# An expert layer of a two-layer model on one core: all 15 row blocks loaded up front, three buffers for the copied weights

## The reference

```python
x = x + ga * _L1_attn_ref(h, ...)
h = _layernorm(x, axis=-1) * (1 + cb) + sb
# _L1_ffn_ref:
router_probs = softmax(xt @ Wr + br)
gates, idx = max(router_probs), argmax(router_probs)      # one of E = 8 experts per token
xn = (xt - mu) * rsqrt(var + LN_EPS) * ln_g + ln_b
h = relu(xn @ W1[idx] + b1[idx])                          # 128 -> 512
y = (h @ W2[idx] + b2[idx]) * gates                       # 512 -> 128
x = x + gb * y
```

## Time and profile before

| | us |
|---|---|
| median of three runs | 1146.57 |
| profiled execution | 1146.85 |
| its span, first to last instruction | 1145.0 |
| TensorE busy | 907.2 |
| DVE busy | 631.0 |
| ACT busy | 518.3 |
| POOL busy | 190.5 |
| first load of xb issued | 967.87 |
| first layer of block 2 / of block 14 starts | 985.77 / 1104.34 |
| first gather starts | 1118.51 |
| mean granted clock | 0.802 |

### The profile page before, as it was taken

One profiled execution on the slowest core, in us unless ns is written; L12 is line 12 of the kernel. 1 busy time (PEld: TensorE's weight loads), 2 busy tenths in 40 slices (PEclk: granted clock), 3 DMA queues, 4 the chain that ended last, 5 costly groups with the idle time before them and its releaser, 6 DMA issues. The chain is left out here.

```text
span 1145.0 us, 13297 instructions
## 1 busy us (share of the span) xinstructions
PE 907.2 (79%) x4532; PEld 524.6 (46%) x4532; DVE 631.0 (55%) x1354; ACT 518.3 (45%) x938; POOL 190.5 (17%) x161
## 2 busy tenths in 40 slices
PE   4559999999889999999968689689789961655550
PEld 2325555556557677776732223223323321555540
DVE  3326576866537675675686357577666514322222
ACT  1014545555557767665725345444444430433330
POOL 3625402121010000000022220010010013122215
PEclk9999999999999999999966556756655555766775
DMA  3414111111191000002112600300200000000003
GB/s 109 74 49 121 33 36 29 41 32 29 52 284 36 1 1 1 1 1 37 19 38 53 100 16 10 49 10 10 48 11 1 2 9 28 10 28 28 28 20 81
DMA packets 55647, 44.80 MB, mean 39 GB/s; under 512 B 5831, under 2 KB 46492, under 8 KB 55580
## 3 DMA queue, kind: packets, MB, share of 16 engines
q1 hardware_dynamic: 54555, 41.86, 15.3%
q0 software_dynamic: 1024, 2.10, 0.6%
HBM read 14.71 MB, written 14.55 MB: 26 GB/s over the span
## 5 line engine op out<-in xcount | busy, mean ns | idle before, releaser
L830 ACT ACTIVATE ring<-single 128x512 f32<-128x512 f32 (+3 forms) x512 | 249.9, 516 | 336.6 <-PE single L1031 190.6
L1445 DVE TENSOR_REDUCE mneg<-pair 128x2 f32<-128x1024 f32 (+3 forms) x256 | 259.5, 1022 | 125.0 <-PE pair L1031 66.6
L1031 PE MATMUL single<-q_op,k_op 26*128 26x512 f32 (+3 forms) x512 | 240.8, 570 | 55.0 <-ACT ring L830 31.8
L1031 PE MATMUL pair<-k_op,q_op 24*128 24x512 f32 (+3 forms) x512 | 210.9, 565 | 24.2 <-DVE mneg L1445 17.8
L1031 PEld LDWEIGHTS single<-q_op,k_op 122*128 122x128 f32 (+1 forms) x512 | 105.7, 237 | 168.3 <-ACT ring L830 82.7
L1088 PE MATMUL p_o<-ring,vaug 128*9 128x512 f32 (+3 forms) x1024 | 160.3, 707 | 1.2 <-ACT ring L830 1.2
L1500 DVE TENSOR_TENSOR ring<-ring,single 128x1024 f32<-128x1024 f32 x60 | 73.2, 1221 | 77.5 <-PE single L1143 62.2
L857 ACT ACTIVATE ring<-pair,cols 128x512 f32<-128x512 f32 x136 | 86.0, 685 | 63.9 <-PE pair L1132 62.4
L1031 PEld LDWEIGHTS pair<-k_op,q_op 120*128 120x128 f32 (+1 forms) x512 | 100.5, 246 | 30.8 <-DVE mneg L1445 23.2
L1505 DVE TENSOR_TENSOR hid_lo<-ring,hid_hi 128x1024 fp32r<-128x1024 f32 x68 | 83.2, 1224 | 10.4 <-ACT hid_hi L872 10.3
L872 ACT ACTIVATE hid_hi<-ring 128x1024 fp32r<-128x1024 f32 x68 | 72.1, 1060 | 12.4 <-issue 7.5
(11 more groups left out here) (286 smaller groups left out, 1412.1 us busy)
## 6 DMA issues: line engine op xcount, KB each, us to landing
xs<-zero SPq DMA_DIRECT2D x10, 1024.0 KB, 10.3
q_op<-hl SPq DMA_DIRECT2D x96, 64.0 KB
k_op<-hl SPq DMA_DIRECT2D x96, 64.0 KB
stage<-in_L_ffn_W_dram SPq DMA_DIRECT2D x8, 512.0 KB, 4.4
stage<-in_L_ffn_rW_dram SPq DMA_DIRECT2D x6, 512.0 KB, 5.8
xb<-xs SPq DMA_DIRECT2D x15, 128.0 KB, 2.0
xs<-yb SPq DMA_DIRECT2D x15, 128.0 KB, 1.7
qk_rope<-rope_hl SPq DMA_DIRECT2D x24, 64.0 KB, 2.0
```

Of the source, the lines that this page charges most:

```text
L830: exp_done.by(act.activation(ring[:, n % 8, lo:T], singles[n % 2][:, lo:T], ACT.Exp), (L, n))
L1031: ins = pe.matmul(dst[:, lo:hi], r32(lhs[:, lhs_lo:lhs_lo + P]), r32(rhs[:, lo:hi]), start=True, stop=L == 1)
L1445: s_taken.by(dve.tensor_reduce(mneg[:, G % 2, qt, 2 * p:2 * p + 2], pairs[m % 2][:, :, 0:hi], axis=AX.X, op=ALU.max, negate=True), (L, m))
```

## The change

SP issues the 15 loads one after another, each into its own part of a larger `xb` and with its own semaphore, and then the 15 stores. The copied weights and bias columns have three buffers in place of two; the third weight buffer lies on `hl`. Tiles at `at_op` move to other offsets, and `yg` moves to where the first rows were.

```diff
@@ placement
+        wst_at = cursor[0] - 8 * KB
-        b_blk = put("b_blk", [P, 2, 5])
+        b_blk = put("b_blk", [P, 3, 5])
-        wst = put("wst", [P, 2, 4, T], at=at_ring)
+        wst = [put("wst0", [P, 4, T], at=at_ring), put("wst1", [P, 4, T], at=at_ring + 8 * KB), put("wst2", [P, 4, T], at=wst_at)]
-        xb = put("xb", [P, 3, 2, D], at=at_op)
+        xb = put("xb", [P, NBLK, 2, D], at=at_op)
...
-        yg = put("yg", [P, NB, NT, D], at=at_op + 35 * KB)
+        yg = put("yg", [P, NB, NT, D], at=at_op)
-        xb_in, yb_out = [sem(f"xb_in{i}") for i in range(3)], [sem(f"yb_out{i}") for i in range(2)]
+        xb_in, yb_out = [sem(f"xb_in{i}") for i in range(NBLK)], [sem(f"yb_out{i}") for i in range(2)]
@@ SP
-            where = {}
-            for n in range(NBLK + 3):
-                if n < NBLK:
-                    where[n] = sp.value_load(btab[0:1, 0, n:n + 1], min_val=0, max_val=79)
-                    if n >= 3:
-                        xt_full.wait_ge(sp, n - 3)
-                    sp.dma_start(xb[:, n % 3, :, :].rearrange("p t d -> p (t d)").unsqueeze(1), blocks_of[:, bass.ds(where[n], 1), :]).then_inc(xb_in[n % 3], 16)
-                if n >= 3:
-                    m = n - 3
-                    yb_ready.wait_ge(sp, m)
-                    sp.dma_start(blocks_of[:, bass.ds(where[m], 1), :], yb[:, m % 2, :, :].rearrange("p t d -> p (t d)").unsqueeze(1)).then_inc(yb_out[m % 2], 16)
+            where = []
+            for n in range(NBLK):
+                where.append(sp.value_load(btab[0:1, 0, n:n + 1], min_val=0, max_val=79))
+                sp.dma_start(xb[:, n, :, :].rearrange("p t d -> p (t d)").unsqueeze(1), blocks_of[:, bass.ds(where[n], 1), :]).then_inc(xb_in[n], 16)
+            for n in range(NBLK):
+                yb_ready.wait_ge(sp, n)
+                sp.dma_start(blocks_of[:, bass.ds(where[n], 1), :], yb[:, n % 2, :, :].rearrange("p t d -> p (t d)").unsqueeze(1)).then_inc(yb_out[n % 2], 16)
@@ POOL
-                if n >= 2:
-                    y_full.wait_ge(pool, n - 2)
-                    yt_ready.wait_ge(pool, n - 2)
+                if n >= 3:
+                    y_full.wait_ge(pool, n - 3)
+                    yt_ready.wait_ge(pool, n - 3)
                     apart(pool)
-                pool.tensor_copy(b_blk[:, n % 2, :].unsqueeze(1), b_cols[:, bass.ds(e, 1), :])
-                w_here.by(pool.tensor_copy(r32(wst[:, n % 2, :, :].unsqueeze(2)), w_of[:, :, bass.ds(e, 1), :]), n)
+                pool.tensor_copy(b_blk[:, n % 3, :].unsqueeze(1), b_cols[:, bass.ds(e, 1), :])
+                w_here.by(pool.tensor_copy(r32(wst[n % 3][:, :, :].unsqueeze(2)), w_of[:, :, bass.ds(e, 1), :]), n)
@@ TensorE, rows_in
-                    pe.wait_ge(xb_in[n % 3], 16 * (n // 3 + 1))
+                    pe.wait_ge(xb_in[n], 16)
...
```

More of the change, by code:

```diff
@@ L319, in build @@
         k_op1 = put("k_op1", [P, 2, NG, T], at=at_op + 32 * KB)
-        xb = put("xb", [P, 3, 2, D], at=at_op)
[L321 to L327, removed]
-        yg = put("yg", [P, NB, NT, D], at=at_op + 35 * KB)
+        xb = put("xb", [P, NBLK, 2, D], at=at_op)
+        xt_hi = put("xt_hi", [P, 2, BLK], at=at_op + 15 * KB)
+        xt_lo = put("xt_lo", [P, 2, BLK], at=at_op + 17 * KB)
+        yt = put("yt", [P, 2, BLK], at=at_op + 19 * KB)
+        yb = put("yb", [P, 2, 2, D], at=at_op + 21 * KB)
+        hid1 = put("hid1", [P, 2, 4, BLK], at=at_op + 23 * KB)
+        hid1_hi = put("hid1_hi", [P, 2, 4, BLK], at=at_op + 31 * KB)
+        hid1_lo = put("hid1_lo", [P, 2, 4, BLK], at=at_op + 39 * KB)
+        yg = put("yg", [P, NB, NT, D], at=at_op)
         at_w = room(2 * 2 * CPR * P * 4)
@@ L902, in hidden @@
                         ins = act.activation(hid1[:, n % 2, c, :], pairs[n % 2][:, c // 2, BLK * (c % 2):BLK * (c % 2) + BLK], ACT.Relu,
-                                             bias=b_blk[:, n % 2, c:c + 1])
+                                             bias=b_blk[:, n % 3, c:c + 1])
                     relu_done.by(ins, n)
@@ L1188, in rows_in @@
                         lo = P * t
-                        ins = pe.transpose(singles[0][:, lo:lo + P], xb[:, n % 3, t, :], ident)
+                        ins = pe.transpose(singles[0][:, lo:lo + P], xb[:, n, t, :], ident)
                     xt_full.by(ins, n)
@@ L1200, in first_layer @@
                         dst = pairs[n % 2][:, c // 2, BLK * (c % 2):BLK * (c % 2) + BLK]
-                        hi, lo = (r32(wst[:, n % 2, half, P * c:P * (c + 1)]) for half in range(2))
+                        hi, lo = (r32(wst[n % 3][:, half, P * c:P * (c + 1)]) for half in range(2))
                         pe.matmul(dst, hi, r32(xt_hi[:, n % 2, :]), start=True, stop=False)
@@ L1212, in second_layer @@
                     for c in range(4):
-                        hi, lo = (r32(wst[:, n % 2, 2 + half, P * c:P * (c + 1)]) for half in range(2))
+                        hi, lo = (r32(wst[n % 3][:, 2 + half, P * c:P * (c + 1)]) for half in range(2))
                         pe.matmul(dst, hi, r32(hid1_hi[:, n % 2, c, :]), start=(c == 0), stop=False)
@@ L1553, in result @@
                     apart(dve)
-                    yt_ready.by(dve.tensor_scalar(yt[:, n % 2, :], (p_o, p_m)[n % 2][:, 0:BLK], b_blk[:, n % 2, 4:5], None, ALU.add), n)
+                    yt_ready.by(dve.tensor_scalar(yt[:, n % 2, :], (p_o, p_m)[n % 2][:, 0:BLK], b_blk[:, n % 3, 4:5], None, ALU.add), n)
                 low_rows(0)
```

## The result

The changed kernel takes **1074.18 us** (median of 3 runs, 1068.37 to 1074.76) against 1146.57 (1134.54 to 1147.28): ratio 0.938, 95% interval 0.928 to 0.949. Its profiled execution took 1074.18 us as well, 72.7 less than the one of before (1146.85), with a span of 1072.4. The forecast was 1078. Times here are medians of all executions of a kernel, and ratios leave out the slow executions, those more than 1.5% above its fastest.

What follows compares the result with a forecast made beforehand. Two waits ending within half a microsecond bounded layer 1's expert blocks: row loads behind late stores, and weight copies. 1146.85 less 3.8 (block 2), 64.3 (12 blocks) and 1.2 (tail) gave 1078 us; range 1064 to 1098.

Steps and rivals of the forecast that it cites:

- part 1: Loads on SP: 15 issues at most 1.14 us apart, no wait for rows left after the first.
- part 2: Three weight buffers: POOL's third copy no longer waits, first layer of block 2 starts at once, 3.8 us gained.
- either alone would give little: Expert blocks of layer 1: row and weight waits end within half a microsecond, so removing one gains little.
- part 3: Expert loop: POOL's copy holds up DVE's xt_lo in each block; 4.52 us a block, 12 blocks 64.3 us less.
- The rival without a lock: Expert loop: POOL's copy rarely holds up xt_lo; 3.94 us a block, 1071 us; chance 0.12.
- The clock: TensorE in the new loop: no idle over about 1.1 us, so 2.4 GHz from block 2 on.
- The low-clock rival: TensorE stays at or falls back to 1.2 GHz: 6.0 us a block, 1096 us; chance 0.18 including mixtures.
- The tail: Last first layer to the gather: one layer of 12 matmuls at the higher clock, 1.2 us less.

Runs made afterwards that it cites:

- lag5: w3_only with the store of block n-5, not n-3, behind the load of block n, still three row buffers: 1077.89 us, ratio 0.939 to the kernel before.
- w3_only: The kernel before with the change's three weight buffers, loads left where they stood: 1132.46 us, ratio 0.989 to the kernel before.
- no_copy: The changed kernel without the copy of block weights from block 3 on (blocks use old weights): 1065.51 us, ratio 0.931 to the kernel before.
- x15_only: The changed kernel with two weight buffers again, the 15 loads still up front: 1145.73 us, ratio 0.998 to the kernel before.
- w4_only: The changed kernel with a fourth weight buffer, xt moved elsewhere in SBUF: 1076.73 us, ratio 0.931 to the kernel before.
- w4_xt_psum: The changed kernel with xt kept in PSUM and a fourth weight buffer: 1069.13 us, ratio 0.933 to the kernel before.
- half_copy: The changed kernel copying only the first layer's weights from block 3 on: 1069.10 us, ratio 0.933 to the kernel before.

## Why the prediction was right

**The rows of the loads and their reach (part 1).** Right: no wait for rows but the first, and 15 issues 1.11 us apart (at most 1.14 was said). The last one was out by 981.8, before the first store had to go. lag5 adds what the step didn't claim: the queue's order was the cause.

**The first layer of block 2 (part 2).** -4.0 against -3.8, without an idle. What w3_only showed is that "either alone would give little" was too low for this one: I had priced the removed waits at block 2 and 14 by themselves, and not what comes sooner because of them.

**What is late next (part 3).** Right in mechanism and size: 4.52 a block, 12 blocks 54.26 us against 54.2. The single held xt_lo of the earlier trace rows was the only case of it in the trace; it held for 12 blocks because the order of copy and xt_lo is decided by yt, 0.81 and 0.96 after it. That the sum is met to a few hundredths is in part luck. In the block from 1015.77 on, the transposes start 0.15 behind xt_lo, the first layer 0.17 behind them and its last matmul 1.38 later, where the sum had 0.05, 0.30 and 1.31; these errors nearly cancel. The rival without a lock, 3.94 a block, is near what no_copy measured (3.86) with the copies out. The mean that was written for it was right, but not its even pace: in no_copy TensorE waits for hid_lo in every second block only, and the blocks take about 3.4 and 4.4 us in turn.

**The clock.** Right: 1.00 from 982 to 1036 with idles of about 1.1 us in each block. The low-clock rival needed 6.0 a block. In x15_only, with idles of 4.35 us, the clock was 0.75, and a first matmul took 0.55 instead of 0.38. So a part of the 64.3 us is the clock that came with the tighter loop: 24 matmuls a block all at 0.12, where part of them ran at 0.22. How large a part, no run separates.

**The tail.** Too small: -2.15 and not -1.2. I gave one layer back to the higher clock. The second layer of block 14, whose first matmul took 0.55 at 1111.50, took 0.38 at 1039.96 behind an idle about as long (2.42 and 2.16 us). What the engine had done before that idle differed: a 12-block loop at 1.00 here, a 5.00 us idle one layer earlier there. That this is the reason is argued, not shown.

**Not foreseen.** The stage began 2.0 us earlier though nothing ahead of it was changed. The total came out 3.8 us under the forecast: 2.0 of this, 1.0 of the tail, 0.2 each of the second and the last stretch, and 0.45 of rounding 1077.55 up to 1078.

## What to carry to other kernels

Before taking away the wait that a profile names, look for the one that ends just behind it: here each removal alone gave 0.2 or 1.1%, both 6.2%. A deep set of buffers can hide that only the order on one queue was wrong: a load should not stand behind a store whose data come so late that the load's rows are already wanted. In lag5 a store two blocks older in the same place cost nothing. When a loop gets tighter, find what then runs under a GpSimd copy on VectorE with two inputs in SBUF: moving one of them to PSUM took 1.6 us from each such instruction, and gave 0.64 us a block once the copies had a fourth buffer.

## What the runs showed of the hardware

- A held VectorE instruction ends a fixed time behind the copy: 0.28 us for 128x256 with copies of 1.04 and of 1.89 us, and in w4_only also where it started 0.62 or 0.52 us into the copy and took 1.54 or 1.65; 1.09 for 128x1024. Alone they take 0.42 and 1.23, so all but 0.14 us of the instruction lies behind the copy. A hid_lo that started 0.15 us before the end of a copy lost nothing (w4_xt_psum, 1.23 us).
- It is the copy that came first in every such case, and no full copy of the expert blocks took over 1.90 us. What a copy does that starts under such a VectorE instruction, no run here shows.
- The stage starts at different times although the instructions ahead of it are the same: its first weight copy at 959.8 us in half_copy, 963.6 in after, 965.6 in before, 967.8 in no_copy and 971.4 in lag5. In the attention of layer 1, from 720 to 955 us, the mean granted clock was 0.58, 0.54 and 0.55 in half_copy, after and no_copy. The first fits the direction and the other two don't order their starts, so the clock there is a part of the cause at most, and the rest is open. This is why totals 5 us apart hardly tell kernels apart here, and the stage does.
- Whether the copy could be avoided altogether, by addressing the block's weights in place, wasn't tried. no_copy shows about what it could give over the changed kernel if the addressing cost nothing: 8.0 us of the stage, and w4_xt_psum has 8.0 already.
